# Key norms of a perceiver block on one core: 16 heads through one product, with a new order of the work

## The chip, the cores and the metric

The kernel runs on 1 core of one Trainium2 chip. The metric is the device time of one execution in microseconds (us), lower is better. TensorE (PE in the profile, its weight loads PEld) multiplies matrices, VectorE (DVE) and ScalarE (ACT) work elementwise, GpSimd (POOL) does too but can't reach PSUM, and SyncE (SP) issues the DMAs. They run beside each other and meet only at semaphores.

## The reference

Sixteen batches of 64 latents attend, with 16 heads of width 128, to a context of 1601 rows of width 128. Then follow a small self attention and a gated attention on the latents, which the change doesn't touch.

```python
q = (hidden_states @ Wq).reshape(B, Sq, H, D)           # B 16, Sq 64, H 16, D 128
k = (encoder_hidden_states @ Wk).reshape(B, Skv, H, D)  # Skv 1601
v = (encoder_hidden_states @ Wv).reshape(B, Skv, H, D)
q = rmsnorm(q, gq)                                      # x * rsqrt(mean(x^2) + 1e-5) * g
k = rmsnorm(k, gk)
scores = jnp.einsum('bqhd,bkhd->bhqk', q, k) * scale
attn = jax.nn.softmax(scores, axis=-1)
out = jnp.einsum('bhqk,bkhd->bqhd', attn, v).reshape(B, Sq, H * D) @ Wo
```

The kernel never forms the keys for the scores. It multiplies the queries by Wk once (the "weighed queries"), so that a score is a product with the context row c itself. What is left of the keys is one number for a row and a head, the norm |c Wk_h|, with which the score is scaled before the exponential. That norm is either the sum of the squares of c Wk_h, or c' G_h c with the Gram matrix G_h = Wk_h Wk_h' (the sum over 128 columns of (c G_h) times c). The values and Wo are applied after the attention.

## The kernel before, in words

Three blocks follow each other: `queries` (the weighed queries, in 32 items of a head and 512 latents, some 130 us), `cross_attention` (some 1220 us) and `self_attentions` (some 160 us).

In `cross_attention` a batch's 1601 context rows are 13 tiles of 124 or 123 rows. The 16 batches make 8 pairs of 26 tiles (TP), so 208 tiles. One step of the software pipeline works on five tiles at once, named by letters: x is turned (PE transpose to `psT`, ACT writes the rounded high part `cTh`, DVE the rest `cTl`), k gets its key norms, r the inverse root of the norms, s its scores, v its weighed sum. All 16 heads of a tile are 2048 columns, in four chunks of 512 (four heads), c = 0 to 3. A product that needs more than the rounded precision is made of 2 or 3 matmuls on rounded parts (high by high, high by low, low by high); these take a rounded type. Where both operands are plain float32 the record shows two matmuls for one.

- `key_chunk(k, c)` on PE fills one of two PSUM banks, `psK[c % 2]`. Chunk 0 is c Wk (3 matmuls), and ACT sums its squares (`squares`). Chunks 1 to 3 are c G (2 matmuls each), and DVE multiplies each with twice the low-corrected context `c2` (`products`). The sums over the columns: ACT for chunk 1 (`product_sums`, four activations with an accumulator read each), DVE for chunks 2 and 3 in one reduce of 1024 columns (`key_sums`).
- `score_half(s, half)`: 3 matmuls of 512 columns into `psS[half]`, which DVE scales by the inverse root (`scale_scores`) into `prob`; ACT takes the exponential in place (`exponentials`), POOL adds it to `acc` (`add`), the softmax denominators before the sum over rows.
- `weigh_half(v, half)`: prob by context into `psO`, accumulated over 13 tiles, plain float32. After a batch `evacuate` takes `psO` out, `denominators` sums `acc` over the rows with a matmul by ones (plain float32, 512 columns a half), and ACT (`logarithms`, `inverses`), DVE (`newton_start`, `newton_end`) and POOL (`normalise`) turn it into a division.
- POOL also makes the parts of the next batch's context and queries (`context_low`, `context_twice_low`, `query_low`), from ACT's (`context_high`, `query_high`), one piece in a step as tables of tile numbers say (HIGH_AT, LOW_AT, TWICE_AT and so on), and four small instructions for the inverse root of a tile (`key_mean`, `key_root`).

Nothing schedules: each engine's order is the order of the calls in its `step`, written by hand, and each wait names a count of a semaphore. The first 9 steps (LAG) and the fill before them (5 steps) are written out, then a loop of 26 steps runs 7 times with a branch back at its end, then the last steps are written out, the drain with `late` work for the matrices Wv Wo among them. `end` has what follows the last tile.

In a step, PE's order is chunk 0, half 0 of the scores, transpose, chunk 1, half 0 of the weighing, chunk 2, half 1 of the scores, chunk 3, half 1 of the weighing. DVE's is scale half 0, products of chunk 1, `cTl`, products of chunk 2, scale half 1, products of chunk 3, the reduce.

## Time and profile before

| what | us |
|---|---|
| median of 3 runs (1528.72 to 1530.05) | 1530.04 |
| the profiled execution, its own time | 1526.53 |
| its span, first to last instruction | 1524.8 |
| busy over the span: PE / DVE / ACT / POOL | 1438.0 / 1300.6 / 1156.1 / 942.6 |
| mean granted TensorE clock, share of full | 0.982 |

The profile describes one execution. 1.7 us of its time lie around the span, and it was 3.5 us faster than the median. The busy times are over the whole; for the stage that matters they are read in windows, and a busy PE is not PE at its peak, since a matmul's record begins before the one ahead has ended. What an instruction costs its engine is therefore read from start to start of neighbours that don't wait.

### The profile page before, as it was taken

To read this page: it belongs to the slowest core of one execution; us is meant where nothing else is said; L and a number is where in the kernel's file an instruction comes from. 1 tells how busy PE (TensorE), PEld (TensorE's weight loads), DVE (VectorE), ACT (ScalarE), POOL (GpSimd) and SP (SyncE) were. 2 spreads that over 40 slices of the span, in tenths; PEclk is the share of its full clock that TensorE was granted. 3 is DMA by queue.
4 is the path that set the end of the run, shared out by engine and by line. 5 is a ranking of instruction groups with operands and counts; after the bars stand their busy time and mean duration, and the time that the engine had idled before them with its cause. 6 is when DMAs were issued, how large, how long until landed. Compare 5 with 4: busy or idle time off the path is not lost. (4 is left out here: it accounts for less than half of the span.)

```text
span 1524.8 us, 29153 instructions
## 1 busy us (share of the span) xinstructions
PE 1438.0 (94%) x6176; PEld 973.3 (64%) x6176; DVE 1300.6 (85%) x2093; ACT 1156.1 (76%) x4810; POOL 942.6 (62%) x1474
## 2 busy tenths in 40 slices
PE   5996999999999999999999999999999999976886
PEld 3664666666666666666666666666666666853554
DVE  6876888998988898889888998988998988765985
ACT  5886888787888887788878787887878877534763
POOL 4001778887878887788878787878887876010000
PEclk9998999999999999999999999999999999996998
DMA  3000000000000000000000000000001011000000
GB/s 139 37 1 1 1 1 23 7 17 17 8 22 2 23 1 22 2 22 1 22 2 22 10 13 21 3 22 2 23 1 47 1 49 42 1 1 0 8 7 15
DMA packets 9818, 25.05 MB, mean 16 GB/s; under 512 B 736, under 2 KB 6016, under 8 KB 9520
## 3 DMA queue, kind: packets, MB, share of 16 engines
q1 hardware_dynamic: 9648, 23.49, 4.3%
q14 instruction: 149, 1.22, 0.3%
q8 instruction: 21, 0.34, 0.1%
HBM read 22.44 MB, written 1.05 MB: 15 GB/s over the span
## 5 line engine op out<-in xcount | busy, mean ns | idle before, releaser
L807 PE MATMUL psK<-wkh,c_cTh 128*124 128x512 f32 x832 | 509.2, 612 | 6.1 <-DVE c_prod L1235 2.8
L1235 DVE TENSOR_TENSOR c_prod<-psK,c_c 124x512 f32<-124x512 f32 x624 | 427.0, 684 | 65.6 <-PE psK L807 61.7
L1529 POOL TENSOR_TENSOR c_acc<-c_acc,c_prob 123x1024 f32<-123x1024 f32 (+1 forms) x192 | 459.1, 2391 | 2.6 <-issue 1.4
L827 PE MATMUL psO<-c_prob,raw 123*128 123x512 f32 (+1 forms) x832 | 424.9, 591 | 0.0
L1021 ACT ACTIVATE c_unused<-c_prod 124x128 f32<-124x128 f32 x832 | 247.5, 299 | 110.5 <-DVE c_prod L1235 110.5
L1252 DVE TENSOR_TENSOR c_prob<-psS,c_ss 124x512 f32<-124x512 f32 x416 | 286.9, 690 | 50.2 <-PE psS L818 34.8
L807 PE MATMUL psK<-wkl,c_cTh 128*124 128x512 f32 x832 | 328.6, 395 | 0.0
L1027 ACT ACTIVATE c_prob<-c_prob,shift 124x1024 f32<-124x1024 f32 x208 | 238.9, 1149 | 56.7 <-DVE c_prob L1252 45.4
L1242 DVE TENSOR_REDUCE c_ss<-c_prod 124x8 f32<-124x1024 f32 x208 | 253.8, 1220 | 7.2
L1013 ACT ACTIVATE c_unused<-psK 124x128 f32<-124x128 f32 x832 | 218.8, 277 | 52.9 <-PE psK L807 37.4
L807 PEld LDWEIGHTS psK<-wkh,c_cTh 128*124 128x124 f32 x832 | 154.4, 186 | 143.6 <-issue 88.7
L807 PEld LDWEIGHTS psK<-wkl,c_cTh 128*124 128x124 f32 x832 | 155.9, 187 | 107.6 <-issue 97.7
L827 PEld LDWEIGHTS psO<-c_prob,raw 123*128 123x128 f32 (+1 forms) x832 | 157.3, 189 | 38.1 <-issue 1.0
L1013 ACT ACTIVATION_READ_ACCUMULATOR c_unused<-psK 124x1 f32 x832 | 172.1, 207 | 0.0
L818 PE MATMUL psS<-c_qwh,c_cTh 128*124 128x512 f32 x416 | 165.1, 397 | 1.1 <-issue 1.1
L818 PE MATMUL psS<-c_qwh,c_cTl 128*124 128x512 f32 x416 | 163.9, 394 | 0.0
L818 PE MATMUL psS<-c_qwl,c_cTh 128*124 128x512 f32 x416 | 163.1, 392 | 0.0
L1021 ACT ACTIVATION_READ_ACCUMULATOR c_unused<-c_prod 124x1 f32 x832 | 155.4, 187 | 0.0
L1443 POOL TENSOR_TENSOR c_low<-raw,c_ch 124x384 f32<-124x384 f32 x64 | 69.4, 1084 | 109.0 <-ACT c_ch L1051 109.0
L1505 POOL TENSOR_SCALAR c_ss<-c_ss 124x16 f32<-124x16 f32 x208 | 50.4, 242 | 125.9 <-DVE c_ss L1242 108.9
L818 PEld LDWEIGHTS psS<-c_qwh,c_cTh 128*124 128x124 f32 x416 | 76.6, 184 | 21.5 <-issue 2.0
L818 PEld LDWEIGHTS psS<-c_qwl,c_cTh 128*124 128x124 f32 x416 | 76.7, 184 | 20.5 <-issue 0.7
(312 smaller groups left out, 2311.5 us busy)
## 6 DMA issues: line engine op xcount, KB each, us to landing
raw<-in_ctx SPq DMA_DIRECT2D x16, 799.5 KB
raw<-in_L_xattn_Wq SPq DMA_DIRECT2D x3, 512.0 KB, 9.7
xs<-in_x SPq DMA_DIRECT2D x1, 1024.0 KB, 5.7
big<-in_L_xattn_Wk SPq DMA_DIRECT2D x1, 1024.0 KB, 9.0
c_prod<-in_L_xattn_Wo SPq DMA_DIRECT2D x1, 1024.0 KB, 5.2
out<-s_y SPq DMA_DIRECT2D x8, 128.0 KB, 1.7
big<-in_L_ffn_W_qkv SPq DMA_DIRECT2D x1, 768.0 KB, 12.9
c_wqkv<-in_L_attn_W_qkv SPq DMA_DIRECT2D x1, 768.0 KB, 15.9
```

What stands on the lines that cost most here:

```text
L807: last = nc.tensor.matmul(psK[0:ROWS, c % 2, :], x[:, slot, :], w[:, cols], start=(n == 0), stop=(n == len(terms) - 1))
L818: last = nc.tensor.matmul(psS[0:ROWS, half, :], x[:, slot, :], w[:, b, cols], start=(n == 0), stop=(n == 2))
L827: nc.tensor.matmul(psO[:, half, :], raw[0:rows, b, tile, :], prob[0:rows, probs(v), half * BANK:(half + 1) * BANK], start=(tile == 0), sto ...
L1013: last = nc.scalar.activation(unused[:, c, j, :], psK[0:ROWS, c % 2, j * D:(j + 1) * D], ACT.Square, accum_out=ss[:, k % 2, 0, h:h + 1])
L1021: last = nc.scalar.activation(unused[:, 1, j, :], prod[:, k % 2, 0, j * CD:(j + 1) * CD], ACT.Copy, accum_out=ss[:, k % 2, 0, h:h + 1])
L1027: nc.scalar.activation(prob[:, probs(s), :], prob[:, probs(s), :], ACT.Exp, bias=T.shift[0:ROWS, :]).then_inc(S.expd, 1)
L1235: nc.vector.tensor_tensor(prod[:, k % 2, c - GRAM, :].rearrange("p (h c) -> p h c", c=CD), psK[0:ROWS, c % 2, :].rearrange("p (h c) -> p h ...
L1242: nc.vector.tensor_reduce(ss[:, k % 2, 0, HB * (GRAM + 1):H], prod[:, k % 2, 1:GRAMS, :].rearrange("p a (h c) -> p (a h) c", c=CD), AX.X, ...
L1252: nc.vector.tensor_tensor(prob[:, probs(s), cols].rearrange("p (h q) -> p h q", q=SQ), psS[0:ROWS, half, :].rearrange("p (h q) -> p h q", ...
L1443: nc.gpsimd.tensor_tensor(low[:, PIECES[piece], :], raw[:, batch % 2, PIECES[piece], :], ch[:, PIECES[piece], :].bitcast(F32), ALU.subtrac ...
L1505: nc.gpsimd.tensor_scalar(ss[:, r % 2, 1, :], ss[:, r % 2, 0, :], 1.0 / D, EPS, ALU.mult, ALU.add).then_inc(R.x, 1)
L1529: nc.gpsimd.tensor_tensor(acc[0:rows, batch % 2, :], acc[0:rows, batch % 2, :], prob[0:rows, probs(s), :], ALU.add).then_inc(S.acc, 1)
```

## The change

- All four chunks are c G. `key_chunk` has 2 matmuls for each, 8 for a tile instead of 9. `queries` makes four Gram chunks instead of three, and the copies of Wk itself into `wkh` and `wkl` are gone.
- Chunks 0 and 2 (heads 0 to 3 and 8 to 11): DVE multiplies, ACT sums (`product_sums`, twice for a tile; `squares` is gone).
- Chunks 1 and 3: DVE multiplies into one new buffer `multiplied` and then reduces its 512 columns (`products_summed`), twice for a tile; `key_sums` is gone.
- The counting semaphores `kmm`, `kprod`, `smm`, `zz` are split, one for each chunk or half. A chunk's bank is free again after the product for chunks 0 and 2, but after the reduce (p1, p3) for chunks 1 and 3.
- `denominators` is two matmuls on rounded parts: ACT copies a half of `acc` to `sum_high`, POOL makes the rest (`sum_low_half`), `unit` is ones in the rounded type.
- The pipeline is one step shorter: in a step the tiles are w, e, s, k, x = t to t + 4, with e in the exponential. The order in a step is new on every engine. PE: transpose x, weigh w, chunk 3 of k, scores of s half 1, chunk 0 of x, scores half 0, chunk 1 of x, denominators where there are some, chunk 2 of x. The inverse root's small steps on POOL are spread around its large ones, and the tables of tile numbers are other.
- The weights of the self attention are loaded later, into space that Wv leaves.

```diff
-                if before_c < GRAM:
-                    pe.wait_ge(S.ksq, done(i, t, GRAM, before_c + 1))
-                else:
-                    pe.wait_ge(S.kprod, done(i, t, GRAMS, before_c - GRAM + 1))
+                    pe.wait_ge(S.p2, done(i, k - 1, 1))      # c == 0
+                if c == 1:
+                    pe.wait_ge(S.p3, done(i, k - 1, 1))
+                if c == 2:
+                    pe.wait_ge(S.p0, done(i, k, 1))
+                if c == 3:
+                    pe.wait_ge(S.p1, done(i, k, 1))
...
+                nc.tensor.matmul(psK[0:ROWS, c % 2, :], cTh[:, slot, :], T.wkh[:, cols], start=True, stop=False)
+                nc.tensor.matmul(psK[0:ROWS, c % 2, :], cTh[:, slot, :], T.wkl[:, cols], start=False, stop=True).then_inc((S.k0, S.k1, S.k2, S.k3)[c], 1)
...
+            def products_summed(i, k, c):
+                dve.wait_ge((S.k1, S.k3)[c // 2], done(i, k, 1))
...
+                nc.vector.tensor_tensor(multiplied[:, :, :], psK[0:ROWS, 1, :].rearrange("p (h c) -> p h c", c=CD), tile, ALU.mult).then_inc((S.m1, S.m3)[c // 2], 1)
+                dve.wait_ge((S.m1, S.m3)[c // 2], done(i, k, 1))
+                nc.vector.tensor_reduce(ss[:, k % 2, 0, HB * c:HB * (c + 1)], multiplied[:, :, :], AX.X, ALU.add).then_inc((S.p1, S.p3)[c // 2], 1)
...
-                nc.tensor.matmul(den_bank(i, batch, half), T.ones[0:ROWS, :], acc[:, batch % 2, half * BANK:(half + 1) * BANK],
-                                 start=True, stop=True).then_inc(S.den, 1)
+                nc.tensor.matmul(den_bank(i, batch, half), unit[0:ROWS, :], sum_high[0:ROWS, cols], start=True, stop=False)
+                nc.tensor.matmul(den_bank(i, batch, half), unit[0:ROWS, :], turned_low[0:ROWS, batch % 2, cols],
+                                 start=False, stop=True).then_inc(S.den, 1)
...
+            def step(i, w, e, s, k, x):        # DVE
                 if k is not None:
-                    products(i, k, GRAM)
+                    products(i, k, 2)
+                if w is not None and w % NT == NT - 1:
+                    evacuate(i, w // NT)
...                                            # cTl of x
+                    products_summed(i, k, 3)
+                if x is not None:
+                    products(i, x, 0)
                 if s is not None:
                     scale_scores(i, s, 1)
+                    scale_scores(i, s, 0)
+                if x is not None:
+                    products_summed(i, x, 1)
```

DVE, one full step of `cross_attention`. Before (c_prob is the scaled scores, c_prod the products, c_ss the sums):

```order
L1252 TENSOR_TENSOR c_prob<-psS,c_ss 124x512
L1235 TENSOR_TENSOR c_prod<-psK,c_c 124x512
L1269 TENSOR_TENSOR c_cTl<-psT,c_cTh 128x124
L1235 TENSOR_TENSOR c_prod<-psK,c_c 124x512
L1252 TENSOR_TENSOR c_prob<-psS,c_ss 124x512
L1235 TENSOR_TENSOR c_prod<-psK,c_c 124x512
L1242 TENSOR_REDUCE c_ss<-c_prod 124x8
```

and DVE's full step now:

```order
L1238 TENSOR_TENSOR c_prod<-psK,c_c 124x512
L1275 TENSOR_TENSOR c_cTl<-psT,c_cTh 128x124
L1247 TENSOR_TENSOR c_multiplied<-psK,c_c 124x512
L1249 TENSOR_REDUCE c_ss<-c_multiplied 124x4
L1238 TENSOR_TENSOR c_prod<-psK,c_c 124x512
L1258 TENSOR_TENSOR c_prob<-psS,c_ss 124x512 x2
L1247 TENSOR_TENSOR c_multiplied<-psK,c_c 124x512
L1249 TENSOR_REDUCE c_ss<-c_multiplied 124x4
```

Seven instructions became nine: a fourth multiplication, and two reduces of 512 columns in place of one of 1024. Each reduce stands right behind the multiplication that it reads.

PE, from the weighing in the middle of a step to the next step. Before:

```order
L827 MATMUL psO<-c_prob,raw 128x512
L807 MATMUL psK<-wkh,c_cTh 124x512
L807 MATMUL psK<-wkl,c_cTh 124x512
L807 MATMUL psK<-wkh,c_cTl 124x512
L818 MATMUL psS<-c_qwh,c_cTh 124x512
L818 MATMUL psS<-c_qwl,c_cTh 124x512
L818 MATMUL psS<-c_qwh,c_cTl 124x512
L850 MATMUL psT<-ident,raw 128x124
L807 MATMUL psK<-wkh,c_cTh 124x512
L807 MATMUL psK<-wkl,c_cTh 124x512
```

and PE's order now, from the start of a step (the first L808, L809 are chunk 3, the second chunk 0):

```order
L850 MATMUL psT<-ident,raw 128x124
L828 MATMUL psO<-c_prob,raw 128x512 x2
L808 MATMUL psK<-wkh,c_cTh 124x512
L809 MATMUL psK<-wkl,c_cTh 124x512
L819 MATMUL psS<-c_qwh,c_cTh 124x512
L819 MATMUL psS<-c_qwl,c_cTh 124x512
L819 MATMUL psS<-c_qwh,c_cTl 124x512
L808 MATMUL psK<-wkh,c_cTh 124x512
L809 MATMUL psK<-wkl,c_cTh 124x512
```

The matmul `psK<-wkh,c_cTl` is gone, both halves of the weighing stand together, and chunk 3 now stands behind them.

## Rows read from the trace of the kernel before

**Rows 1.** Windows of the middle: busy us (instructions) of each engine, granted clock, DMA.
```profile
500.00:800.00 300.00, 299.17 (x1114) 199.48 (x1112) 268.36 (x406) 242.25 (x1144) 242.53 (x381) 1.00 0.03 12
```
**Rows 2.** Timeline of PE, a plain step: start us, length us, instruction.
```profile
702.45 0.27 PE L850 MATMUL psT<-ident,raw 124*128 124x124 f32 x1
...
702.80 0.39 PE L807 MATMUL psK<-wkl,c_cTh 128*124 128x512 f32 x1
703.03 1.02 PE L827 MATMUL psO<-c_prob,raw 123*128 123x512 f32 x2
...
704.12 0.40 PE L807 MATMUL psK<-wkl,c_cTh 128*124 128x512 f32 x1
...
707.75 0.27 PE L850 MATMUL psT<-ident,raw 124*128 124x124 f32 x1
```
**Rows 3.** Timeline of DVE around the same step.
```profile
701.25 1.22 DVE L1242 TENSOR_REDUCE c_ss<-c_prod 124x8 f32<-124x1024 f32 x1
702.39 0.68 DVE L1434 SCALAR_TENSOR_TENSOR c_den<-c_den 128x512 f32<-128x512 f32 x1
702.99 0.68 DVE L1252 TENSOR_TENSOR c_prob<-psS,c_ss 124x512 f32<-124x512 f32 x1
...
705.85 0.68 DVE L1235 TENSOR_TENSOR c_prod<-psK,c_c 124x512 f32<-124x512 f32 x1
706.57 1.22 DVE L1242 TENSOR_REDUCE c_ss<-c_prod 124x8 f32<-124x1024 f32 x1
707.95 0.69 DVE L1252 TENSOR_TENSOR c_prob<-psS,c_ss 124x512 f32<-124x512 f32 x1 [0.17 <-PE psS L818]
```
**Rows 4.** Timeline of DVE at two of the loop's branches back: idle time and its releaser in brackets.
```profile
638.19 0.69 DVE L1252 TENSOR_TENSOR c_prob<-psS,c_ss 124x512 f32<-124x512 f32 x1 [2.09 <-PE psO L827]
...
639.40 0.28 DVE L1269 TENSOR_TENSOR c_cTl<-psT,c_cTh 128x124 fp32r<-128x124 f32 x1
639.59 0.68 DVE L1235 TENSOR_TENSOR c_prod<-psK,c_c 124x512 f32<-124x512 f32 x1
...
780.52 0.69 DVE L1252 TENSOR_TENSOR c_prob<-psS,c_ss 124x512 f32<-124x512 f32 x1 [2.06 <-PE psO L827]
```
**Rows 5.** Timeline of PE, a chunk that waited for its bank.
```profile
639.54 0.49 PE L807 MATMUL psK<-wkh,c_cTh 128*124 128x512 f32 x1 [0.31 <-DVE c_prod L1235]
639.87 0.39 PE L807 MATMUL psK<-wkl,c_cTh 128*124 128x512 f32 x1
```
**Rows 6.** Timeline of ACT: an exponential, and product sums of one head each.
```profile
700.66 1.15 ACT L1027 ACTIVATE c_prob<-c_prob,shift 124x1024 f32<-124x1024 f32 x1 [0.40 <-DVE c_prob L1252]
...
704.61 0.29 ACT L1021 ACTIVATE c_unused<-c_prod 124x128 f32<-124x128 f32 x1
...
704.91 0.29 ACT L1021 ACTIVATE c_unused<-c_prod 124x128 f32<-124x128 f32 x1
```
**Rows 7.** Timeline of POOL, the large addition and a side piece.
```profile
706.84 1.30 POOL L1497 TENSOR_TENSOR big<-big,c_den 128x512 f32 x1
...
708.39 2.40 POOL L1529 TENSOR_TENSOR c_acc<-c_acc,c_prob 123x1024 f32<-123x1024 f32 x1
```
**Rows 8.** Timeline of ACT in the queries: two items apart, then one with a Gram chunk.
```profile
38.13 0.60 ACT L462 ACTIVATE q_square<-psK 128x512 f32<-128x512 f32 x1 [0.16 <-PE psK L393]
...
44.46 0.60 ACT L462 ACTIVATE q_square<-psK 128x512 f32<-128x512 f32 x1 [0.16 <-PE psK L393]
...
49.16 0.60 ACT L462 ACTIVATE q_square<-psK 128x512 f32<-128x512 f32 x1 [1.91 <-PE psK L393]
```
**Rows 9.** Timeline of PE, fill and end of the tiles.
```profile
139.14 0.44 PE L850 MATMUL psT<-ident,raw 124*128 124x124 f32 x1 [6.21 <-SPq L766]
...
161.66 0.27 PE L850 MATMUL psT<-ident,raw 124*128 124x124 f32 x1
...
1284.93 1.88 PE L827 MATMUL psO<-c_prob,raw 123*128 123x512 f32 x4
1287.11 1.12 PE L836 MATMUL psM<-c_acc,ones 124*128 124x512 f32 x2 [0.29 <-POOL c_acc L1529]
```

More of the change, by code:

```diff
@@ L239, in gram_at @@
         def gram_at(n):
-            return [q for q in range(GRAM, KC) if n == 8 + 4 * (q - GRAM)]
+            return [q for q in range(KC) if n == 4 + 4 * q]
         def turn_bank(j):
@@ L710, in steps @@
             for t in range(LAG, TP if last else TP + LAG):
-                yield tuple(u if not last or u < TP else None for u in (t, t + 2, t + 3, t + 4, t + 5))
+                yield tuple(u if not last or u < TP else None for u in range(t, t + 5))
         def pipeline(eng, emit, end=None, begin=None):
-            for t in range(-5, LAG):
-                emit(0, *(u if u >= 0 else None for u in (t, t + 2, t + 3, t + 4, t + 5)))
-                if begin is not None and t < 0:
-                    begin(t + 5)
+            for t in range(-4, LAG):
+                if begin is not None and t < 1:
+                    begin(t + 4)
+                emit(0, *(u if u >= 0 else None for u in range(t, t + 5)))
             with eng.Fori(0, NPAIR - 1) as i:
@@ L727, in pipeline, with sums_at @@
                 end(NPAIR - 1, 1)
+        def sums_at(w, table):
+            for half, n in enumerate(table):
+                if w is not None and w % NT == n % NT and w >= n % NT + (NT if n >= 0 else 0):
+                    yield (w // NT if n < 0 else w // NT - 1), half
         def late(i, v):
@@ L969, in end @@
             def end(i, batch):
+                denominators(i, batch, 0)
                 pe.wait_ge(W.vTl, 2)
@@ L1025, in exponentials @@
[L1025 to L1027 removed]
+                last.then_inc((S.a0, S.a2)[c // 2], 1)
+            def exponentials(i, e):
+                act.wait_ge(S.z1, done(i, e, 1))
+                act.wait_ge(S.z0, done(i, e, 1))
+                nc.scalar.activation(prob[:, probs(e), :], prob[:, probs(e), :], ACT.Exp, bias=T.shift[0:ROWS, :]).then_inc(S.expd, 1)
@@ L1029, in key_log, with sum_high_half @@
+            def sum_high_half(i, batch, half):
+                cols = slice(half * BANK, (half + 1) * BANK)
+                act.wait_ge(S.acc, done(i, NT * (batch + 1) - 1, 1))
+                act.wait_ge(S.den, batch_done(i, batch - 1, 2))
+                nc.scalar.activation(sum_high[0:ROWS, cols], acc[:, batch % 2, cols], ACT.Copy).then_inc(S.acch, 1)
             def key_log(i, r):
-                act.wait_ge(S.ksum, done(i, r, 1))
-                act.wait_ge(S.ksq, done(i, r, GRAM))
@@ L1051, in context_high, with step @@
                 nc.scalar.activation(ch[:, PIECES[piece], :], raw[:, b, PIECES[piece], :], ACT.Copy).then_inc(S.nath, 1)
-            def step(i, v, s, r, k, x):
-                e = s - 1 if s is not None and s > 0 else TP - 1 if s is None and v == TP - 2 else None
+            def step(i, w, e, s, k, x):
+                for batch, half in sums_at(w, SUM_HIGH_AT):
+                    sum_high_half(i, batch, half)
+                if late(i, w) == 3:
+                    sum_high_half(i, 1, 1)
+                if x is not None:
+                    act.wait_ge(S.ct, done(i, x, 1))
+                    act.wait_ge(S.s0, done(i, x - before(CT_SLOT, x), 1))
+                    nc.scalar.activation(cTh[:, CT_SLOT[x % TP], :], psT[:, 0:ROWS], ACT.Copy).then_inc(S.cth, 1)
                 if e is not None:
@@ L1058, in step @@
                 if k is not None:
[L1059 to L1082 removed]
+                    product_sums(i, k, 2)
+                if w is not None:
+                    if w % NT in QUERY_HIGH_AT and more(i, w // NT + 1):
+                        query_high(i, w // NT + 1, QUERY_HIGH_AT.index(w % NT))
+                    for piece in pieces_at(i, w, HIGH_AT):
+                        context_high(i, *piece)
+                    if w % NT == NT - 1:
+                        evacuate(i, w // NT)
+                if k is not None:
+                    key_log(i, k)
+                for batch, half in sums_at(w, LOG_AT):
+                    logarithms(i, batch, half)
+                for batch, half in sums_at(w, INVERSE_AT):
+                    inverses(i, batch, half)
+                if k is not None:
+                    key_guess(i, k)
+                if x is not None:
+                    product_sums(i, x, 0)
+                l = late(i, w)
                 if l == 0:
@@ L1217, in begin @@
                     context_high(0, 0, 0)
-                if n in (1, 2):
-                    query_high(0, 0, n - 1)
+                    nc.scalar.activation(unit[:, :], T.ones[:, :], ACT.Copy).then_inc(W.unit, 1)
+                if n == 1:
+                    for half in range(2):
+                        query_high(0, 0, half)
                 if n in (2, 3, 4):
@@ L1448, in context_twice_low @@
                 pool.wait_ge(S.nat, batch_done(i, batch, len(PIECES), piece + 1))
-                pool.wait_ge(S.kprod, done(i, NT * (batch - 1) + PIECES[piece].stop - 1, GRAMS))
+                for sem in (S.p0, S.p1, S.p2, S.p3):
+                    pool.wait_ge(sem, done(i, NT * (batch - 1) + PIECES[piece].stop - 1, 1))
                 nc.gpsimd.tensor_tensor(c2[:, PIECES[piece], :], raw[:, batch % 2, PIECES[piece], :], low[:, PIECES[piece], :],
@@ L1484, in begin @@
                     context_twice_low(0, 0, 0)
-                if n in (1, 2):
-                    query_low(0, 0, n - 1)
+                if n == 1:
+                    for half in range(2):
+                        query_low(0, 0, half)
                 if n in (2, 3, 4):
```

276 lines of the change are left out of this document (117 added, 159 removed).

## Prediction, written before the changed kernel was run

> **What bounds the kernel now.** I read the windows first. In the middle of the tiles PE is busy in 299.2 of 300 us, DVE in 268.4, ACT in 242.3, POOL in 242.5, at the full granted clock of 2.4 GHz [rows 1]. Since a matmul's record overlaps the next, I went to PE's timeline and read from start to start. A matmul on rounded parts with 512 columns costs 0.23 us (702.80 to 703.03). A half of the weighing, plain float32, costs 0.86 (703.03 to 704.12 less 0.23 for the chunk matmul between). The transpose costs 0.12 (702.45 to 702.80 less 0.23). So a step needs 15 x 0.23 + 2 x 0.86 + 0.12 = 5.29, and the transposes are 5.30 apart (702.45 to 707.75) [rows 2]: PE waits for nothing, it is the bound. DVE has room. Its 512-column instruction costs 0.60 (702.39 to 702.99), also behind the reduce. The reduce of 1024 columns costs 1.14 (701.25 to 702.39), and where an instruction reads what the one ahead wrote it starts 0.72 behind it, not 0.60 (705.85 to 706.57) [rows 3]. `cTl` costs 0.19 (639.40 to 639.59) [rows 4]. DVE's step is thus 5 x 0.60 + 0.12 + 1.14 + 0.19 = 4.45, and it waits for PE (the bracket at 707.95) [rows 3].
>
> A pair of 26 tiles takes 142.33 (638.19 to 780.52) [rows 4]. That is 26 x 5.30 = 137.80, four denominators at 0.86 = 3.44, and 1.09 left, which is the branch back: every engine stops there, DVE for 2.1 us [rows 4], of which the room on DVE gives a half back.
>
> **PE's part of the change.** A step loses one matmul: 14 x 0.23 + 1.72 + 0.12 = 5.06. Denominators cost 2 x 0.23 = 0.46 instead of 0.86. If PE stayed the bound, this were the gain: 208 x 0.23 + 32 x 0.40 = 61 us.
>
> **DVE's part.** A step now has four multiplications, two scalings, two reduces and `cTl`. A reduce of 512 columns isn't in the trace. From `cTl` (124 columns, 0.28) and the product (512 columns, 0.68) a column costs 0.0010 us, 512 of them 0.53, so the reduce of 1024 less 512 columns is 1.14 - 0.53 = 0.61. Bounds from the same rows: half of 1.14, 0.57, and a whole product with the wait behind, 0.72. I take 0.60, the price of every other 512-column instruction. Each of two reduces waits for its product, 0.12 more. The step is 8 x 0.60 + 2 x 0.12 + 0.19 = 5.23. This is above PE's 5.06, so DVE becomes the bound, and PE's saving is worth nothing from there on.
>
> **The round trip.** DVE's last instruction of a step is the reduce of chunk 1 (p1). PE's chunk 3 waits for it, since it fills the same bank, and DVE's third instruction of the next step waits for chunk 3. A chunk that waited: product at 638.80 ends 639.48 (start 0.60 ahead of 639.40, length 0.68), PE starts at 639.54, its second matmul at 639.87, which ends 0.39 later at 640.26 [rows 4, 5]. With 0.04 until DVE sees it the trip is 0.06 + 0.33 + 0.39 + 0.04 = 0.82. DVE covers 0.60 + 0.19 of it with its first two instructions, less the 0.08 by which they start ahead of the reduce's end: 0.71. So 0.11 is left, and a plain step is 5.34. Is PE there in time? From chunk 3 on it needs 0.56 + 0.69 + 0.46 + 0.69 + 0.46 + 0.46 + 0.12 + 1.72 = 5.16 until it stands at chunk 3 again, so it waits 0.18 and the trip is cold each time. The other bank waits (p2, p3, p0) come by my walk through the step 0.05 to 0.4 ahead of PE. Bounds of this term: 0 (PE loads the weights ahead) and 0.33 (trip fully cold and nothing covered but `cTl` and half a product).
>
> **What stands between.** In a batch DVE has four instructions for the denominators and one evacuation, at 0.60 each. A step with one hides the trip: 0.60 - 0.11 = 0.49 more. Branches back: DVE now pays the stop in full, 2.1 instead of 1.09. A step with a first half of denominators makes PE's row 5.16 + 0.46 = 5.62 against 5.34, 0.28 more (the second halves fall on steps in which DVE has an extra instruction).
>
> **The other engines.** ACT trades four squares for four product sums, at 0.30 a head [rows 6]. Its step: 8 x 0.30, the exponential with 1.15 to 1.3, three small ones about 0.6, and side pieces about 0.5 on the mean: 4.8. POOL's step: the addition 2.4, five small ones with their waits about 1.3, and nearly each step a side piece of 1.0 to 1.3 [rows 7], two of them new: 4.9 to 5.0. Both stay below 5.34, by little. I price their wait at 0 and keep 0.2 a step as the upper bound.
>
> **The sum over the tiles,** from the first transpose, 139.14, to the end of the last weighing, 1286.7: 1147.5 us [rows 9]. Before, that is 203 full steps at 5.30 = 1075.9, 30 denominators = 25.8, 6 branches = 6.5, and 39.3 for the fill (22.5, 139.14 to 161.66 [rows 9]) and the drain (16.8). Now 204 full steps at 5.34 = 1089.4; 75 further DVE instructions (60 and 15) at 0.49 = 36.8; 15 denominators at 0.28 = 4.2; 6 branches at 2.1 = 12.6. The fill is one step shorter, but its steps are fuller: about 20. The drain has one full step less of PE work: about 14. Together 1177, so 29.5 more.
>
> **Outside.** One more Gram chunk: an item with one took 4.70 (44.46 to 49.16), two without took 6.33 (38.13 to 44.46) [rows 8], so 1.5. The copies that go were beside PE's work: 0. At the end of the tiles the denominators now wait for ACT's copy and POOL's rest, 0.6 + 1.3 behind the last addition, and for the second half 1.3 more; they started 1287.11 and PE had a wait of its own behind them [rows 9]. I take 1.5, bounds 0 and 3.5. The later load of the self attention's weights has some 30 us before its first reader: 0, and some 5 if it came late. Self attention itself: 0.
>
> Sum: 29.5 + 1.5 + 1.5 = 32.5, less some 2 because my steps are rounded up to hundredths throughout (two of 0.12 for 0.11 to 0.12): 30. The profiled execution would go from 1526.5 to 1556.5. It was 3.5 under the median of the runs, so the median goes from 1530 to about 1560.
>
> **A rule against it.** The trace prices a wait for the instruction ahead on DVE at 0.12 us [rows 3]. The Trainium skill says otherwise ("VectorE: DVE Perf Modes", section "The DRAIN you can't avoid"): a next instruction starts only when the pipe is empty, and a semaphore between two costs nothing extra. No pair here bears that out: 0.60 stands against 0.72 at the same size. What a free wait would give is the second rival.
>
> **Rivals.**
> 1. DVE is the bound but the trip is hidden, because PE loads the weights ahead or waits less. 0.11 x 204 less 0.11 x 75 = 14 less: 1546. For it: PE's row is 0.18 short of DVE's only. Against: the chunk in rows 5 waited cold, with both matmuls after the semaphore. 0.2.
> 2. Faster than before: the two waits cost nothing, at the place product to reduce. DVE's step is 4.99 + 0.11 = 5.10, 0.24 less over 204 steps, 49 us: 1511. It decides the sign from 5.20 a step on (30 / 204 = 0.15 less). Against: the 0.72 in every tile. That PE stays the bound altogether (1530 - 61 + 3 = 1472) would need DVE to do nine instructions in what eight and a half take. 0.05 for both.
> 3. ACT or POOL get late as well: three engines within some tenths of each other, each waiting for the other inside a step (a product sum for DVE's product, `cTh` behind four product sums, POOL's small instructions behind a side piece and the addition). Half of the bound, 0.1 a step over 208, is 21: 1581; the whole is 1602. For it: POOL's wait times now are room (57 of 300 us) [rows 1], which goes. Against: each of these results is needed only a step later. 0.2.
> 4. The edges cost no more than before (a branch at 1.09, fill shorter by a whole step): 6 + 3 less, 1551. It lies inside the range.
>
> **Numbers.** Forecast 1560 (0.5, with the edges' variant), rival 1 0.2, rival 3 0.2, rival 2 0.05, 0.05 for what I haven't seen. About 3 us, 0.2%, is what can be told from no change. Slower 0.91, same 0.04 (between rivals 1 and 2), faster 0.05. Range: down past rival 1 with the shorter edges, 1537; up past the middle of rival 3, 1588.
>
> **What would show it.** DVE busy over 95% of the middle windows and PE below 97%, with idle time ahead of chunk 3 put down to the reduce; transposes 5.3 to 5.4 apart in plain steps; the reduce of 512 columns with 0.68 and 0.72 behind its product; at the branch back DVE idle 2.1. Wrong would be: transposes 5.1 apart (the waits are free), reduces clearly off 0.60, or DVE idle with ACT or POOL as releaser (rival 3).

## The result, and the profile after

| | before | changed | ratio (95% interval) |
|---|---|---|---|
| median of 4 runs each, same chip, us | 1529.38 | 1565.16 | 1.0244 (1.0224 to 1.0264) |
| the profiled execution, us | 1526.53 | 1565.89 | |
| its span | 1524.8 | 1564.0 | |
| mean granted clock, share of full | 0.982 | 0.975 | |

The change makes the kernel slower by 36 us, where 30 were forecast (1560, range 1537 to 1588).

The window in the middle of the tiles, same columns as [rows 1]:

```profile
500.00:800.00 300.00, 296.10 (x1026) 174.62 (x1025) 287.96 (x497) 247.35 (x1113) 245.50 (x373) 0.99 0.03 12
```

DVE went from 268 to 288 us, PE did 1026 instructions where it did 1114, and still shows 296 us busy, not the 291 or less that the prediction asked for. That number misleads. A matmul's record is longer than what it costs (in the weighing 0.59, and they start 0.43 apart), so it covers a short wait behind it, and the record of a matmul that starts behind a wait is longer still (0.49 in place of 0.39). The timeline shows the wait. Here is a plain step of PE in the changed kernel, from one transpose to the next, which answers to [rows 2]:

```profile
702.93 0.27 PE L850 MATMUL psT<-ident,raw 124*128 124x124 f32 x1
703.04 1.88 PE L828 MATMUL psO<-c_prob,raw 123*128 123x512 f32 x4
704.87 0.49 PE L808 MATMUL psK<-wkh,c_cTh 128*124 128x512 f32 x1
705.20 0.39 PE L809 MATMUL psK<-wkl,c_cTh 128*124 128x512 f32 x1
705.43 0.40 PE L819 MATMUL psS<-c_qwh,c_cTh 128*124 128x512 f32 x1
...
708.26 0.27 PE L850 MATMUL psT<-ident,raw 124*128 124x124 f32 x1
```

The transposes are 5.33 apart (forecast 5.34; 59 of the 207 steps measure 5.33 or 5.34, 16 more 5.35). Chunk 3 starts at 704.87, its second matmul 0.33 later, as behind the wait in [rows 5], where 0.23 is the distance without one. The prediction called this a cold trip. What chunk 3 waited for is the reduce, in DVE's timeline of the same step, which answers to [rows 3]:

```profile
703.42 0.68 DVE L1247 TENSOR_TENSOR c_multiplied<-psK,c_c 124x512 f32<-124x512 f32 x1
704.13 0.69 DVE L1249 TENSOR_REDUCE c_ss<-c_multiplied 124x4 f32<-124x512 f32 x1
704.73 0.68 DVE L1238 TENSOR_TENSOR c_prod<-psK,c_c 124x512 f32<-124x512 f32 x1
705.33 0.27 DVE L1275 TENSOR_TENSOR c_cTl<-psT,c_cTh 128x124 fp32r<-128x124 f32 x1
705.63 0.69 DVE L1247 TENSOR_TENSOR c_multiplied<-psK,c_c 124x512 f32<-124x512 f32 x1
706.36 0.69 DVE L1249 TENSOR_REDUCE c_ss<-c_multiplied 124x4 f32<-124x512 f32 x1
706.96 0.68 DVE L1238 TENSOR_TENSOR c_prod<-psK,c_c 124x512 f32<-124x512 f32 x1
```

Read from start to start: the reduce of 512 columns occupies DVE for 0.60 (704.13 to 704.73) and starts 0.71 to 0.73 behind its product. The reduce ends at 704.82, PE starts 0.05 later. `cTl` costs 0.30 here (705.33 to 705.63), not 0.19: the 0.11 is the end of the trip from DVE to PE and back, DVE waiting for chunk 3. The waits say the same in sums over 600 us (engine and line that waited, releaser, us in total, times, longest):

```profile
PEld psK L808 <- DVE c_ss L1249: 88.6, 148, 0.8
...
PEld psK L808 <- DVE c_cTl L1275: 27.3, 45, 2.5
...
PEld psK L808 <- DVE c_prod L1238: 22.9, 89, 0.3
...
DVE c_prod L1238 <- issue: 12.4, 5, 2.6
```

PE waited for DVE, most often for the reduce, and DVE's own longest line is that of the branches back, 2.5 each. None of its idle time has ACT or POOL as releaser.

The stages, each as profiled, in us:

| | before | changed | difference | forecast |
|---|---|---|---|---|
| up to the first transpose | 139.14 | 141.53 | +2.4 | +1.5 |
| first transpose to the end of the last weighing | 1147.5 | 1180.7 | +33.2 | +29.5 |
| from there to the matrices Wv Wo | 2.7 | 4.5 | +1.8 | +1.5 |
| the rest | | | +2.0 | 0, less 2 for rounding |
| sum | | | +39.4 | +30 |

The sum is 39.4 and not 36 because the profiled execution of the kernel before was 2.9 under its median, and that of the changed kernel 0.7 over its own.

The marks of the end of the tiles, PE, which answer to [rows 9]:

```profile
1320.52 1.88 PE L828 MATMUL psO<-c_prob,raw 123*128 123x512 f32 x4
1324.90 0.50 PE L839 MATMUL psM<-c_sum_high,c_unit 124*128 124x512 f32 x1 [2.49 <-POOL c_turned_low L1541]
```

### The profile page after: what moved, and what is told of

It reads as the page before. It is cut to its first block and busy times, and to the rows that moved or that the text cites. A ratio compares the mean times of both kernels' runs of the same rounds, so it can differ in the third digit from the quotient of the medians.

```text
span 1564.0 us, 29049 instructions
## 1 busy us (share of the span) xinstructions
PE 1467.0 (94%) x5980; PEld 903.2 (58%) x5980; DVE 1414.5 (90%) x2510; ACT 1211.5 (77%) x4843; POOL 989.3 (63%) x1505
## 5 line engine op out<-in xcount | busy, mean ns | idle before, releaser
L1014 ACT ACTIVATE c_unused<-c_prod 124x128 f32<-124x128 f32 x1664 | 493.4, 298 | 138.9 <-DVE c_prod L1238 134.6
L808 PE MATMUL psK<-wkh,c_cTh 128*124 128x512 f32 x832 | 386.7, 465 | 15.8 <-DVE c_cTl L1275 13.7
L828 PE MATMUL psO<-c_prob,raw 123*128 123x512 f32 (+1 forms) x832 | 392.6, 594 | 0.0
L809 PE MATMUL psK<-wkl,c_cTh 128*124 128x512 f32 x832 | 331.2, 398 | 0.0
L808 PEld LDWEIGHTS psK<-wkh,c_cTh 128*124 128x124 f32 x832 | 153.9, 185 | 287.4 <-DVE c_ss L1249 176.6
L1014 ACT ACTIVATION_READ_ACCUMULATOR c_unused<-c_prod 124x1 f32 x1664 | 311.1, 187 | 0.0
L1238 DVE TENSOR_TENSOR c_prod<-psK,c_c 124x512 f32<-124x512 f32 x416 | 283.0, 680 | 17.4 <-issue 14.9
L1249 DVE TENSOR_REDUCE c_ss<-c_multiplied 124x4 f32<-124x512 f32 x416 | 285.4, 686 | 14.3
L1247 DVE TENSOR_TENSOR c_multiplied<-psK,c_c 124x512 f32<-124x512 f32 x416 | 283.9, 682 | 9.9 <-PE psK L809 6.7
L1258 DVE TENSOR_TENSOR c_prob<-psS,c_ss 124x512 f32<-124x512 f32 x416 | 265.6, 680 | 0.0
L809 PEld LDWEIGHTS psK<-wkl,c_cTh 128*124 128x124 f32 x832 | 156.5, 188 | 12.0 <-issue 0.5
L1032 ACT ACTIVATE c_ss<-c_ss,eps 124x16 f32<-124x16 f32 x208 | 63.4, 305 | 46.5 <-DVE c_ss L1249 45.3
L819 PEld LDWEIGHTS psS<-c_qwh,c_cTl 128*124 128x124 f32 x416 | 77.0, 185 | 19.9
## 6 DMA issues: line engine op xcount, KB each, us to landing
big<-in_L_ffn_W_qkv SPq DMA_DIRECT2D x1, 768.0 KB, 12.4
```

The costliest lines, as they stand in the source:

```text
L808: nc.tensor.matmul(psK[0:ROWS, c % 2, :], cTh[:, slot, :], T.wkh[:, cols], start=True, stop=False)
L809: nc.tensor.matmul(psK[0:ROWS, c % 2, :], cTh[:, slot, :], T.wkl[:, cols], start=False, stop=True).then_inc((S.k0, S.k1, S.k2, S.k3)[c], 1)
L819: last = nc.tensor.matmul(psS[0:ROWS, half, :], x[:, slot, :], w[:, b, cols], start=(n == 0), stop=(n == 2))
L828: nc.tensor.matmul(psO[:, half, :], raw[0:rows, b, tile, :], prob[0:rows, probs(v), half * BANK:(half + 1) * BANK], start=(tile == 0), sto ...
L1014: last = nc.scalar.activation(unused[:, j, :], prod[:, k % 2, c // 2, j * CD:(j + 1) * CD], ACT.Copy, accum_out=ss[:, k % 2, 0, h:h + 1])
L1238: nc.vector.tensor_tensor(prod[:, k % 2, c // 2, :].rearrange("p (h c) -> p h c", c=CD), psK[0:ROWS, 0, :].rearrange("p (h c) -> p h c", c ...
```

## The experiments

All ratios are to the kernel before, on the same chip. A difference between two experiments is worked out from their ratios times 1528. A plain step is one without an extra DVE instruction (the evacuation or one of the four Newton instructions of a batch), without denominators and without a branch back. "The branch back" stands for the step that has it, from transpose to transpose.

**The changed kernel again**, as reference of the first set.

> The changed kernel again, so that the others of this set have it on their own chip. 1565 us, ratio 1.024 to before.

Measured: 1568.2 (1563.3 to 1568.8), ratio 1.0245 (1.0224 to 1.0266), as the first time.

**The round trip.**

```diff
 if c == 1:
-    pe.wait_ge(S.p3, done(i, k - 1, 1))
+    pe.wait_ge(S.m3, done(i, k - 1, 1))
...
 if c == 3:
-    pe.wait_ge(S.p1, done(i, k, 1))
+    pe.wait_ge(S.m1, done(i, k, 1))
```

> The changed kernel, but PE's chunks 1 and 3 wait for the product that read their bank (m1, m3), no longer for the reduce behind it (p1, p3). Nothing else moves, DVE has the same instructions in the same order. Theory (the round trip PE to DVE shows 0.11 us in each step, because chunk 3 may start only behind the reduce): chunk 3 starts 0.6 to 0.7 us earlier, the trip is covered, a plain step falls from 5.34 to 5.23 us, DVE waits for nothing inside a step. 0.11 x (204 - 75) = 14 us less than the changed kernel: about 1551, and still some 20 slower than before. Rival (the 0.11 is DVE's own, or ACT's and POOL's releases stand behind it at once): 1562 to 1566. Rival (PE is the bound, DVE merely looks busy): no change.

Measured: 1554.2, ratio 1.0164 (1.0147 to 1.0181), 12.4 less than the changed kernel. Plain steps are 5.22 to 5.23 apart in place of 5.34. The term of 0.11 and its place are right, and both rivals fall.

**Is DVE the bound? Half of the columns in the reduces.**

```diff
-nc.vector.tensor_reduce(ss[...], multiplied[:, :, :], AX.X, ...)
+nc.vector.tensor_reduce(ss[...], multiplied[:, :, 0:CD // 2], AX.X, ...)
```

> The changed kernel with both reduces on half of the columns (64 of each head's 128; the norms then lack the other half, so the output is not the reference's). DVE's step falls by 2 x 0.26 = 0.53 us to 4.70, PE's 5.06 stays. Theory (DVE bounds the tiles): PE becomes the bound; DVE's excess of 0.28 over PE's 5.06 goes in 204 steps (57 us), the extra DVE instructions go with it (75 x 0.49 = 37, less 31 x 0.46 for the denominators that PE now pays = 14), branches back 1 us each: 1565 - 57 - 37 + 14 - 5 = about 1480. Rival 3 of the prediction (ACT and POOL are late by themselves once DVE is quick, with their 4.8 and 4.9 a step, side pieces on top): 1500 to 1520. Rival (PE bound already in the changed kernel): 1565.

Measured: 1503.8, ratio 0.984 (0.9824 to 0.9857), 62 less. Plain steps are 5.06 to 5.08, PE's 5.06 of the prediction: PE is the bound once DVE has less to do. DVE bounded the changed kernel. My figure of 1480 was 24 too low. The long steps tell why:

```profile
709.56 0.68 DVE L1238 TENSOR_TENSOR c_prod<-psK,c_c 124x512 f32<-124x512 f32 x1
710.16 0.68 DVE L1265 COPY big<-psO 128x512 f32 x1
710.75 0.28 DVE L1275 TENSOR_TENSOR c_cTl<-psT,c_cTh 128x124 fp32r<-128x124 f32 x1
```

The extra DVE instruction does not go for free even with DVE's step at 4.70. Most such steps are 5.2 to 5.5 (5.7 with denominators), some 15 us over plain ones in all once PE's own part for the denominators is taken off. In 14 of them the extra instruction itself took 0.87 in place of 0.68, beside one of POOL's; more of that below. The branch back still takes 7.4 to 8.3 in place of 5.07, 16 for the six, where the figure of 1480 had 1 us each. These two make the 24. For the extras I read it so, not tested by itself: DVE's step of 4.70 with 0.60 more is 5.30, which is above PE's 5.07, and PE stands at most two banks ahead of DVE, so the slack of the steps around it does not make that good. 1480 had spread the slack evenly.

**Is PE's time hidden?**

```diff
-nc.tensor.matmul(psK[0:ROWS, c % 2, :], cTh[:, slot, :], T.wkl[:, cols], start=False, stop=True).then_inc(...)
+last = nc.tensor.matmul(psK[0:ROWS, c % 2, :], cTh[:, slot, :], T.wkl[:, cols], start=False, stop=(c != 0))
+if c == 0:
+    last = nc.tensor.matmul(psK[0:ROWS, c % 2, :], cTl[:, slot, :], T.wkh[:, cols], start=False, stop=True)
+last.then_inc(...)
```

> The changed kernel with the third matmul of chunk 0 back (cTl by the high part of its columns; the norms of four heads are thereby slightly other than c'Gc of the change). PE's step is 0.23 us longer, 5.29 in place of 5.06, DVE's is as it was. Theory (DVE bounds, PE waits 0.28 a step): most of the 0.23 is hidden in PE's waits, but 5.29 is then within 0.05 of DVE's 5.34, and steps with a first half of denominators or a warm chunk 3 pass it: 0 to 10 us more, 1565 to 1575. Rival (PE bounds): 208 x 0.23 = 48 more, 1613.

Measured: 1583.1, ratio 1.0345 (1.0321 to 1.037), 15 more, above my 0 to 10 and far from 48. Most plain steps are 5.38 to 5.54. The prediction's own row gives it: from chunk 3 to chunk 3, with a cold start, PE needs 5.16, and with 0.23 more 5.39, above DVE's 5.34. I had compared the 5.29 of a PE that never waits.

**The denominators alone**, in the kernel before.

```diff
-nc.tensor.matmul(den_bank(i, batch, half), T.ones[0:ROWS, :], acc[:, batch % 2, half * BANK:(half + 1) * BANK], ...)
+nc.tensor.matmul(den_bank(i, batch, half), unit[0:ROWS, :], sum_high[0:ROWS, cols], start=True, stop=False)
+nc.tensor.matmul(den_bank(i, batch, half), unit[0:ROWS, :], turned_low[0:ROWS, batch % 2, cols], start=False, stop=True)
```

> The kernel before (its order, its chunk 0 with three matmuls and squares, its one reduce of 1024 columns), with the denominators alone taken from the changed kernel: ACT's rounded copy of half a sum, POOL's rest, two rounded matmuls in place of the plain float32 one, the changed kernel's tables of places, and its later load of the self attention's weights. PE stays the bound with 5.30 a step and pays 0.46 in place of 0.86 for each of 32 denominators: 32 x 0.40 = 13 us less, 1.5 given back behind the last addition, so about 1518 (ratio 0.992). Rival (in the changed kernel the denominators are what costs: POOL's and ACT's new pieces delay additions and small sums): 1530 or more. Rival (the branch back eats it, since DVE and PE now share the stop): 1522 to 1526.

Measured: 1523.7, ratio 0.9972 (0.9963 to 0.9982). Faster, by 4 us and not by 12. The steps with a denominator fell from 6.17 to 5.77, the 0.40 as priced, and the last transpose comes 9.9 us earlier (1255.68, before 1265.57). Ten steps, one or two in most pairs, are 5.52 to 5.57 in place of 5.30 and take part of it back. In each of them DVE's last Newton instruction took 1.5 in place of 0.68, and a chunk waits for its bank:

```profile
478.97 1.53 DVE L1454 SCALAR_TENSOR_TENSOR c_den<-c_den 128x512 f32<-128x512 f32 x1
```

POOL was at an instruction on two tiles of SBUF, as in the case of `newton_end` below. Behind the tiles another 5.5 are lost. PE waits 2.50 and 0.60 us for the rests, as in the changed kernel, and the granted clock falls there. How much of the 5.5 is the wait and how much the clock was not separated. The windows of this kernel and of the one before, which hold nearly the same work:

```profile
1275.00:1300.00 25.00, 21.90 (x96) 17.32 (x95) 20.67 (x26) 17.13 (x29) 7.70 (x5) 0.93 0.13 43
```
```profile
1285.00:1310.00 25.00, 24.15 (x114) 18.63 (x114) 21.67 (x30) 17.77 (x30) 4.92 (x3) 1.00 0.03 11
```

In that stretch matmuls of 256 columns start 0.21 apart:

```profile
1281.97 0.41 PE L915 MATMUL psK<-c_qwh,c_turned_low 128*128 128x256 f32 x1
1282.18 0.41 PE L915 MATMUL psK<-c_qwh,c_turned 128*128 128x256 f32 x1
```

In the kernel before they start 0.12 apart. This is the lower of the two levels (1.2 GHz, a mean of 0.93 over the window) after some 3 us of waits. In the changed kernel the same waits left the clock at full (0.12 apart at 1326.75), so this is not a sure price of the edit.

**The same arithmetic in the old order**, with one reduce of 1024 columns.

```diff
 # DVE, in a step
+products(i, k, 0)
 scale_scores(i, s, 0)
-products(i, k, GRAM)
-cTl
-products(i, k, 2)
-scale_scores(i, s, 1)
-products(i, k, 3)
+products(i, k, 1)
+products(i, k, 2)
+cTl
+products(i, k, 3)
+scale_scores(i, s, 1)
 key_sums(i, k)          # the reduce
```

> The same arithmetic as the changed kernel, except that the last 8 heads' products (chunks 2 and 3) lie in `prod` and one reduce of 1024 columns sums them, as before; PE's order is that of the kernel before, DVE's is product 0, scaling 0, products 1 and 2, cTl, product 3, scaling 1, reduce, so no instruction of DVE reads what the one ahead of it wrote. DVE's step is 6 x 0.60 + 0.19 + 1.14 = 4.93 against 5.23 in the changed kernel, PE's 5.06 as there. Theory (the changed kernel lost because the two halved reduces with their waits and the trip put DVE's row 0.28 above PE's): step 5.06 to 5.15, some 0.2 to 0.28 less in 204 steps than 5.34, so 1565 less 40 to 57: 1508 to 1525, faster than the kernel before. Rival (c'Gc for all heads costs by itself: ACT's products, POOL's sums, any order): 1545 to 1570.

Measured: 1537.2, ratio 1.0058 (1.004 to 1.0076), between theory and rival. Plain steps are 5.06 to 5.10 as the theory had it, so c'Gc for all heads costs nothing by itself. The 1537 has other causes. The branch back takes 8.15 to 9.9, 23 over plain steps for the six. And the steps with an extra DVE instruction are up to 6.43. Here is one of the longest, DVE with POOL's instruction between:

```profile
703.34 1.21 DVE L1249 TENSOR_REDUCE c_ss<-c_prod 124x8 f32<-124x1024 f32 x1
704.40 0.99 POOL L1457 TENSOR_TENSOR c_c<-raw,c_low 124x384 f32<-124x384 f32 x1 [0.16 <-POOL c_low L1450]
704.47 1.47 DVE L1441 SCALAR_TENSOR_TENSOR c_den<-c_den 128x512 f32<-128x512 f32 x1
705.86 0.68 DVE L1242 TENSOR_TENSOR c_prod<-psK,c_c 124x512 f32<-124x512 f32 x1
```
```profile
706.60 0.49 PE L811 MATMUL psK<-wkh,c_cTh 128*124 128x512 f32 x1 [1.04 <-DVE c_prod L1242]
```

The reduce with an extra behind it is one block in which DVE frees no bank, from 702.82 to 706.54, and PE waits 1.04. But most of that is the length of the extra itself, 1.47 for what took 0.68 in [rows 3]. Where the extra behind the same reduce took 0.68, PE waits some 0.25 and the step is 5.62, 0.54 over a plain one (6.09 to 6.31 with denominators, of which PE's own part is 0.46). The long kind comes 14 times and costs some 0.8 each, 11 us in all. So of the 34 us by which this kernel lies above the fastest one below (1504.0), which has the same plain step within 0.01, the branches are some 16 and the long extras 11; the block of the reduce is what is left. What makes a branch back dearer here was not found.

**The reduce a little behind its product**, with the banks freed early.

```diff
 # DVE, in a step
 products(i, k, 2)
 cTl
-products_summed(i, k, 3)
+reduce(i, k, 1)
+multiply(i, k, 3)
 products(i, x, 0)
+reduce(i, k, 3)
 scale_scores(i, s, 1)
 scale_scores(i, s, 0)
-products_summed(i, x, 1)
+multiply(i, x, 1)
```

> The changed kernel with PE's bank waits of e1_bank (on the product) and each reduce at least one instruction behind its product: DVE's step is product 2, cTl, reduce of chunk 1 (of the tile begun a step ahead), product and sum buffer of chunk 3, product 0, reduce 3, the two scalings, product 1. DVE's instructions are the same 8 x 0.60 + 0.19, the two waits of 0.12 for the instruction ahead are gone: 4.99 a step, below PE's 5.06. Theory (the waits cost 0.24 a step, and nothing else is as late): step 5.06, e1_bank's 1554 less 0.16 x 204 = 33, about 1521. Rival (the buffer `multiplied` holds one product, and the sum of chunk 1 comes a step part later, so ACT's logarithm and POOL's root are late for the scaling): 1530 to 1554.

Measured: 1543.1, ratio 1.0094 (1.0077 to 1.0111). 11 less than with the banks alone, where 33 were hoped for: the rival's range. Plain steps are 5.04 to 5.23, half of them at 5.16 or less, and not 5.06. The cause stands in DVE's timeline:

```profile
704.67 0.67 DVE L1251 TENSOR_REDUCE c_ss<-c_multiplied 124x4 f32<-124x512 f32 x1
705.45 0.69 DVE L1245 TENSOR_TENSOR c_multiplied<-psK,c_c 124x512 f32<-124x512 f32 x1
```

With one buffer, the product of chunk 3 overwrites what the reduce ahead of it reads, and waits for it: 0.78 in place of 0.60. The wait was moved, not removed: DVE's row is 4.99 + 0.18 = 5.17, which is the plain step. So the rival's first half, the one buffer, is shown. Its second half, sums that come too late for the scaling, is not needed for plain steps; over the whole it was not separated.

**The wait for the instruction ahead, taken away** (rival 2 of the prediction made true).

```diff
-dve.wait_ge((S.m1, S.m3)[c // 2], done(i, k, 1))
-nc.vector.tensor_reduce(ss[...], multiplied[:, :, :], AX.X, ...)
+dve.wait_ge((S.p0, S.p2)[c // 2], done(i, k, 1))
+nc.vector.tensor_reduce(ss[...], prod[:, k % 2, c // 2, :], AX.X, ...)
```

SyncE's load of Wo waits for the last reduce too, since that now reads `prod`. The eight heads of chunks 1 and 3 get other heads' sums, so this kernel and the next one price the wait and don't compute what the reference does.

> The changed kernel, in which each reduce of 512 columns reads the product buffer `prod` that DVE filled at least two instructions ahead, not `multiplied` that it filled with the instruction ahead: the same instructions, sizes and order, PE's bank waits as they are, but nothing on DVE waits for the instruction ahead of it. (Eight heads then get the sum of other heads, so the norms and the output are other than the reference's.) This is rival 2 of the prediction made true. Theory (a wait for the instruction ahead costs 0.12 us, twice a step): DVE's step is 4.99, with the trip 5.10, against 5.34; 0.24 less in 204 steps and 75 extra DVE instructions at 0.49 as before: 1565 less 49 = 1516, or, if the trip grows to some 0.2 because PE's own row of 5.16 from chunk 3 to chunk 3 is now the longer, 1565 less 0.17 x 204 = 1530. Rival (the wait costs nothing, the 0.72 between product and reduce is the reduce's own start): 1565, and the reduce still 0.72 behind its product.

Measured: 1511.0, ratio 0.9881 (0.9864 to 0.9897), 56 less than the changed kernel. Rival 2 had said 1511. DVE's timeline now has the reduce at the price of any other neighbour:

```profile
704.52 0.69 DVE L1248 TENSOR_TENSOR c_multiplied<-psK,c_c 124x512 f32<-124x512 f32 x1
705.13 0.68 DVE L1250 TENSOR_REDUCE c_ss<-c_prod 124x4 f32<-124x512 f32 x1
705.72 0.68 DVE L1239 TENSOR_TENSOR c_prod<-psK,c_c 124x512 f32<-124x512 f32 x1
```

0.61 behind the product, where 0.71 to 0.73 stood. Plain steps are 5.04 to 5.25, half of them at 5.11 or less (5.10 was forecast).

Not all of the 56 is the wait. The six steps with a branch back went from 7.6 to 9.0 down to 6.15 to 6.46, because DVE stopped there for 1.25 to 1.55 in place of 2.4 to 2.6:

```profile
769.06 0.69 DVE L1239 TENSOR_TENSOR c_prod<-psK,c_c 124x512 f32<-124x512 f32 x1 [1.35 <-issue]
```

That is some 9 us beyond what a plain step gained, and no run shows why the stop is shorter. The other 47 are the wait's, 0.23 in 204 steps; the changed kernel less 47 is 1518, still under the kernel before. With the early banks as well:

> e8_free and the bank waits of e1_bank together: no wait for the instruction ahead on DVE, and PE's chunks 1 and 3 released by the product. DVE's step 4.99, PE's 5.06. Theory: PE is the bound in plain steps as in e7_half, whose plain step was 5.07; each extra DVE instruction costs 0.52 (4.99 + 0.60 - 5.07) against 0.41 measured in e7_half's; 1565 less 0.27 x 204 = 1510, and 75 x 0.03 = 2 more: 1512. Rival (both engines nearly equal, each stalls the other through the two banks, as in e6_gram_den): 1525 to 1540. Rival (the waits cost nothing): 1554 as e1_bank.

Measured: 1504.0, ratio 0.9835 (0.9818 to 0.9851). 8 under the 1512 of the theory, which had left the branches as they were; they take 6.1 to 6.4 here too. Plain steps are 5.05 to 5.10, most of those with an extra DVE instruction 5.5 to 5.57. With 512 columns reduced it is as fast as with 256 above. PE bounds the plain steps of both; that the totals agree is in part chance, since the kernel above pays more for its branches and less for its extras. I take 1504 as the floor for this order of the work.

**A kernel that keeps the arithmetic and has no such wait.** DVE reduces chunks 0 and 2, ACT sums 1 and 3.

```diff
 # DVE, in a step
 products(i, k, 2)                # into one of two reduce buffers
 cTl
-products_summed(i, k, 3)         # product, then its reduce
-products(i, x, 0)
+products(i, k, 3)                # for ACT
+products_reduced(i, k, 2)
+products(i, x, 0)
 scale_scores(i, s, 1)
 scale_scores(i, s, 0)
-products_summed(i, x, 1)
+products(i, x, 1)                # for ACT
+products_reduced(i, x, 0)
```

> What e9_free_bank only priced, made a kernel that computes all that the reference does: the heads of chunks 0 and 2 are summed by DVE's reduces, those of chunks 1 and 3 by ACT, the other way round than in the changed kernel. DVE's order is product 2, cTl, product 3, reduce 2, product 0, the two scalings, product 1, reduce 0, so each reduce reads a product that DVE made at least one other instruction earlier (two buffers of 512 columns for them), and PE's bank is free after each product. ACT sums chunk 1 ahead of chunk 3 in the step after. Theory: same step as e9_free_bank (5.07 plain, 5.55 with an extra DVE instruction), 1504, ratio 0.984, against 1565 of the changed kernel and 1528 before. Rival (ACT gets the last product 0.8 us later than in the changed kernel, its logarithm and POOL's root come too late for the scaling): 0.1 to 0.2 a step more, 1525 to 1545.

Measured: 1517.9, ratio 0.9933 (0.9916 to 0.995). Faster than both kernels, and 15 short of the floor. Forecast were 1504, and 1525 to 1545 by the rival. The plain steps are there (5.04 to 5.15, forecast 5.07). One step in each batch (14 in the trace) is 6.28 in place of 5.57. It holds the second Newton instruction, `newton_end`. DVE, then POOL:

```profile
547.31 1.39 DVE L1441 SCALAR_TENSOR_TENSOR c_den<-c_den 128x512 f32<-128x512 f32 x1
548.63 0.68 DVE L1242 TENSOR_TENSOR c_multiplied<-psK,c_c 124x512 f32<-124x512 f32 x1
```
```profile
547.14 1.01 POOL L1458 TENSOR_TENSOR c_c<-raw,c_low 124x384 f32<-124x384 f32 x1
548.11 0.67 POOL L1528 TENSOR_TENSOR c_ss<-c_ss 124x16 f32<-124x16 f32 x1
```

Both instructions read two tiles of SBUF. POOL's started first and ended at 548.15. DVE's started 0.17 behind it and ended 0.55 after it. POOL's next one, of 16 columns, then took 0.67 in place of 0.22. The last experiment tests whether one holds the other up.

```diff
-HIGH_AT, LOW_AT, TWICE_AT = (5, 7, 10, 14), (6, 8, 11, 15), (6, 10, 14, 16)
+HIGH_AT, LOW_AT, TWICE_AT = (5, 7, 10, 14), (6, 8, 11, 15), (7, 10, 14, 16)
```

> e10_cross with one number of a table changed: POOL makes the first piece of c2 a step later (with tile 7 in place of 6 of a batch). In e10_cross DVE's last Newton instruction of the second half, which reads two tiles of SBUF (`den` and `den`), took 1.39 us instead of 0.68, 14 times of 28 in 1000 us; each time POOL was at an instruction on two SBUF tiles (c2 from raw and low, 1.01 us) when it started, and the step was 6.28 in place of 5.57. Theory (DVE's instruction with two SBUF inputs stands still until POOL's has ended): the later piece leaves POOL free there, the step falls to 5.57, 16 x 0.71 = 11 less, 1507. Rival (these steps are long for another reason, ACT's sums for example, and the long record is only its picture): no change, 1518. A third possibility is that the piece meets another instruction of DVE a step later: between the two.

Measured: 1508.5 (1508.1 to 1510.4), ratio 0.9873 (0.9856 to 0.9891), 9 less, forecast 11. The long steps are 5.56 to 5.58. DVE's group over 1000 us, of this kernel and of the one ahead of it (times, busy us, mean ns, idle):

```profile
L1441 DVE SCALAR_TENSOR_TENSOR c_den<-c_den 128x512 f32<-128x512 f32 x28 | 19.1, 681 | 0.0
```
```profile
L1441 DVE SCALAR_TENSOR_TENSOR c_den<-c_den 128x512 f32<-128x512 f32 x28 | 29.0, 1035 | 0.0
```

Now it is POOL that stands still. Its small instruction beside DVE's takes 0.62 in place of 0.20, and nobody waits for it:

```profile
545.61 0.62 POOL L1533 TENSOR_SCALAR c_ss<-c_ss 124x16 f32<-124x16 f32 x1 [0.20 <-POOL c_ss L1528]
```

This is the fastest kernel here that computes what the reference does: 1.3% under the kernel before, 3.6% under the changed one.

## Why the prediction was right, point by point

- **PE's step 5.06.** Right: 5.06 to 5.08 where DVE did not bound (halved reduces, free waits).
- **DVE's step 5.23 = 8 x 0.60 + 2 x 0.12 + 0.19.** Right in each piece: the reduce 0.60, the wait 0.11 to 0.13, and 5.21 to 5.24 measured once the trip was gone. That DVE is the bound is shown from both sides: less for DVE took 62 us off, 0.23 more a step for PE cost 15 and not 48.
- **Trip 0.11, plain step 5.34.** Right, 5.33 to 5.35. The experiment gave 12.4 us for my 14. The 0.04 until DVE sees PE's end, for which the prediction shows no row, is there as well: chunk 3 ends at 705.59 and DVE starts at 705.63.
- **The wait for the instruction ahead, 0.24 a step.** Shown as a cause: without it 56 us less, of which some 9 came from the branches. The 47 left turn the change from slower to faster by themselves. That rival 2's 1511 was hit to the microsecond is partly luck: it had 49 for the waits, started from 1560 and not 1565, and had nothing for the branches. The Trainium skill ("VectorE: DVE Perf Modes", section "The DRAIN you can't avoid") has the semaphore at no extra cost. At this size the runs differ: 0.71 to 0.73 with it, 0.60 without, start to start.
- **75 extra instructions at 0.49, first halves at 0.28.** Right. Single steps are 5.82, or 5.34 + 0.48. A first half of denominators makes 5.75 to 5.78 and the step behind it 5.12 to 5.14, together 0.2 over two plain ones. For a pair of 26 tiles the terms make 26 x 5.34 + 10 x 0.49 + 2 x 0.28 + 2.1 = 146.4; of the six pairs behind the first, four take 146.5 to 146.8 and two, with the longest branches back, 147.7.
- **Branches back, 2.1 each.** Too small. The six steps are 8.40, 9.01, 7.65, 7.61, 7.62 and 7.77, together 16.0 over plain ones, forecast 12.6. DVE is idle for 2.5 there, not 2.1:

```profile
655.09 0.69 DVE L1238 TENSOR_TENSOR c_prod<-psK,c_c 124x512 f32<-124x512 f32 x1 [2.44 <-issue]
```

- **Fill about 20, drain about 14.** The fill took 21.6, the drain 13. With the branches this makes the tiles' 33.2 for my 29.5.
- **Outside.** Gram chunk and what else lies ahead of the tiles +2.4 for 1.5, the end of the tiles +1.8 for 1.5. The later load cost nothing that shows. The last 2.0 came behind it, where the windows show a lower granted clock over the last 75 us (0.88, before 0.92); nothing in the edit touches that stage. The executions of the kernel before differ by more than this among themselves: 1526.2 to 1526.5 at a mean clock of 0.981 to 0.983 (the profiled one was of these), 1529.7 and above at 0.976 to 0.979. So the 2.0 need not be the change's.
- **Less 2 for rounding.** Wrong: my steps were not rounded up.
- **Rival 3, ACT or POOL late.** Did not come: no wait of DVE for either.
- **The sign to look for in PE, busy below 97%.** A bad sign, as told above: 98.7%. Starts of neighbours are the measure.

36 for 30 is thus one mechanism as forecast, with the edges too cheap. Between the two profiled executions it is 39.4 for 30: 3.7 in the tiles (branches and fill over, drain under), 1.2 ahead of and behind them, 2 for the rounding, 2.0 in the last stage. Of these 9, between 3 and 4 are the choice of executions.

## What to carry to other kernels

When the bound moves from one engine to its neighbour, price the neighbour's step by its starts, with each wait for the instruction ahead as its own term. The order on one engine decided the sign here: as written the change is 2.4% slower than before. With each reduce one other instruction behind its product, two buffers for that and the banks freed by the products, the same arithmetic is 0.7% faster, and 1.3% with one piece of POOL's moved as well. These edits went in together; the wait alone was priced in a kernel that mixes up the heads. If two engines share two banks and their steps are within 5% of each other, an extra instruction of 0.60 that comes now and then is paid at 0.4 to 0.6 here (5.07 to 5.49 and 5.55, 5.22 to 5.82), whatever slack the mean step shows. Read the branch back of a loop from each kernel's own trace: the same 26 tiles had it at 1 to 5 us over a plain step. Before DVE gets an instruction with two SBUF inputs, look at what POOL does at that time.
